# Expert tiles in pairs through Strassen's block product, in a Mamba and mixture-of-experts kernel

## The reference, cut to what matters

```python
E, TOP_K, D, M = 8, 2, 512, 1792
topk_w, topk_idx = jax.lax.top_k(router_probs, TOP_K)
topk_w = topk_w / jnp.sum(topk_w, axis=-1, keepdims=True)
x_rep_sort = jnp.take(x_flat, sort_idx // TOP_K, axis=0)      # rows sorted by expert
h = jax.lax.ragged_dot(x_rep_sort, w1, group_sizes)           # [8192, 512] x [512, 1792]
h = jax.nn.silu(h) * jax.lax.ragged_dot(x_rep_sort, w3, group_sizes)
out_sort = jax.lax.ragged_dot(h, w2, group_sizes)             # [8192, 1792] x [1792, 512]
out = jnp.einsum('tkd,tk->td', out_rep, topk_w)
```

## Time and profile before

| what | value |
|---|---|
| three runs, us | 4488.01, 4486.12, 4482.16; median 4486.12 |
| profiled execution: span from first to last instruction | 4487.7 us; no time of its own is listed beside the span |
| PE busy | 4104.8 us, 91% |
| DVE busy | 2421.6 us, 54% |
| ACT, POOL busy | 1941.3 us, 1849.3 us |
| mean granted clock of TensorE | 0.964 |
| last phase | from 2440.8 us, the first weight load |

### The profile page before, as it was taken

The page is one execution under the profiler, slowest core; times in us unless marked ns, Lnnn a source line. Parts: engine busy times, 40 slices in busy tenths (PEclk is TensorE's granted clock), DMA queues, the critical chain, the costliest instruction groups (busy, mean ns, idle before and its releaser), DMA issues. The chain is left out here.

```text
span 4487.7 us, 70319 instructions
## 1 busy us (share of the span) xinstructions
PE 4104.8 (91%) x25764; PEld 3331.3 (74%) x25764; DVE 2421.6 (54%) x3215; ACT 1941.3 (43%) x4096; POOL 1849.3 (41%) x1394
## 2 busy tenths in 40 slices
PE   6677889989898889898976999999999999999998
PEld 5565677767777677777764888888888888888887
DVE  5999999999999999999994000000000000000000
ACT  7677777877777777777761000000000000000000
POOL 3667777887787777876862000000000000000000
PEclk8888999999999999999987999999999999999999
DMA  4112454454535454545344113030301303030300
GB/s 155 63 61 67 143 163 159 126 168 158 173 117 166 160 170 122 162 157 177 106 141 158 30 25 101 14 112 14 112 14 20 107 14 112 14 112 14 112 14 12
DMA packets 289338, 452.00 MB, mean 101 GB/s; under 512 B 15856, under 2 KB 183408, under 8 KB 280816
## 3 DMA queue, kind: packets, MB, share of 16 engines
q1 hardware_dynamic: 272928, 413.27, 28.2%
q0 software_dynamic: 14768, 34.41, 4.1%
q10 hardware_dynamic: 1440, 1.81, 0.1%
HBM read 920.96 MB, written 45.95 MB: 215 GB/s over the span
## 5 line engine op out<-in xcount | busy, mean ns | idle before, releaser
L625 POOL TENSOR_TENSOR hs<-hs,bc 128x1024 f32<-128x1024 f32 x512 | 1215.1, 2373 | 308.7 <-DVE hs L1337 286.7
L1337 DVE TENSOR_TENSOR_SCAN hs<-dA,pU 128x1024 f32<-128x1024 f32 x512 | 1168.6, 2282 | 49.4 <-ACT dA L744 27.1
L1822 ACT ACTIVATE gate<-pA 128x512 f32<-128x512 f32 x216 | 117.5, 544 | 1859.9 <-PE pB L1860 1859.9
L1738 POOL DMA_INDIRECT out<-ow,trow x54 | 83.7, 1551 | 1967.3 <-DVE ow L1908 1967.3
L744 ACT ACTIVATE dA<-delta,aneg 128x255 f32<-128x255 f32 x2048 | 852.4, 517 | 37.4 <-DVE hs L1337 35.1
L1860 PE MATMUL pA<-xT,w1s 128*128 128x128 f32 x6048 | 799.7, 275 | 0.7 <-ACT xT L1831 0.7
L1860 PE MATMUL pB<-xT,w3s 128*128 128x128 f32 x6048 | 799.5, 275 | 0.0
L1136 PE MATMUL pY<-ident,hs 128*128 128x128 f32 x4096 | 565.1, 286 | 237.0 <-POOL hs L625 236.6
L1860 PEld LDWEIGHTS pA<-xT,w1s 128*128 128x128 f32 x6048 | 741.0, 192 | 26.4 <-issue 25.4
L1136 PEld LDWEIGHTS pY<-ident,hs 128*128 128x128 f32 x4096 | 487.8, 147 | 344.3 <-POOL hs L625 170.4
L1860 PEld LDWEIGHTS pB<-xT,w3s 128*128 128x128 f32 x6048 | 736.9, 192 | 0.0
(11 more groups left out here) (285 smaller groups left out, 3596.5 us busy)
## 6 DMA issues: line engine op xcount, KB each, us to landing
w1s<-in_w SPq DMA_DIRECT2D x165, 1024.0 KB
w3s<-in_w SPq DMA_DIRECT2D x165, 1024.0 KB
w2s<-in_w SPq DMA_DIRECT2D x165, 1024.0 KB
ew<-in_w SPq DMA_DIRECT2D x273, 512.0 KB, 4.1
win<-in_w_in SPq DMA_DIRECT2D x128, 512.0 KB, 4.7
bc<-bc_d SPq DMA_DIRECT2D x64, 1024.0 KB, 11.0
w1s<-in_w SPq DMA_DIRECT2D x55, 512.0 KB
w3s<-in_w SPq DMA_DIRECT2D x55, 512.0 KB
```

The source lines that it names most:

```text
L625: pool.tensor_tensor(hs[b][:, :, :], hs[b][:, :, :], bc[:, N + g * PN:N + (g + 1) * PN, :], ALU.mult)\
L1337: dve.tensor_tensor_scan(hs[b][:, :, :].rearrange("p n t -> p (n t)"), dA[b][:, :, :].rearrange("p n t -> p (n t)"), pU[:, :, :].rearrange ...
L1822: act.activation(gate[q % 2][:, 0:n, :], pA[q % 2][:, 0:n, :], ACT.Silu).then_inc(silu, 1)
```

## The change

With more than one tile of an expert left, two tiles (256 rows) are computed together by Strassen's product in Winograd's form. The matrices are cut in two by two blocks. Up, for each of `JN` = 7 steps of 256 hidden columns: the left matrix has w1's part above w3's, each cut at half of D; the right one has the two tiles, cut the same way. Down: the hidden halves by tile against w2, cut at 128 hidden rows and at half of D. Seven block products take the place of eight, and 15 block sums are added: four on each operand, seven on the products.

- VectorE makes the sums on weights (`combine_up`, `combine_down`; some in place, so w3s and w2s are overwritten and every pair reloads its expert's weights), the seven sums out of PSUM (`gather`, once for each step up and once down), and silu(h) times the other half (`multiply`).
- GpSimd makes the sums on the hidden values (`combine_h`) and on the turned rows (`combine_x`), and issues two indirect DMAs a pair.
- ScalarE copies the first product M1 out of PSUM, computes the silu in place in SBUF, and puts the row weights on the result.
- PSUM holds two sets of four banks: step j of the up part uses set j % 2, the down part set 1, the turned rows set 0.
- The last odd tile of an expert goes into a second loop behind all pairs, which works as the kernel before does, with its own semaphores and with weights loaded anew for each tile. Its first loads stand in SyncE's queue behind the whole last pair.
- The plan has two lists, pairs (at least 22, at most 29) and odd tiles (at most 8).

```diff
-NT_SURE = 2 * TOKENS // P - EARLY
-NT = NT_SURE + E - 1
+LEFT = 2 * TOKENS // P - EARLY
+NP_SURE = -(-(LEFT - E) // 2)
+NP_MAX = (LEFT + E - 1) // 2
+NPS = NP_MAX + 1
...
+KH, DH, JN = DC // 2, D // 2, MK // 2
+TURN_AFTER = 3
...
+            def combine_h(t, j):
+                k = JN * t + j
+                pool.wait_ge(h_mul, k + 1)
+                pool.tensor_tensor(hs[:, j, 0, :], hT[:, j, 2, :], hT[:, j, 3, :], ALU.add).then_inc(hs_step, 1)
...
+            def pair(t):
+                for j in range(JN):
+                    combine_h(t, j)
+                combine_x(t + 1)
+                add_rows(t)
...
+            def pair(t):
+                r, e, new = slot(t + 1)
+                for q in range(NQ):
+                    sp.wait_ge(up_mm, JN * t + min(2 * q + 2, JN))
+                    load_up(q, e, w13_in, new)
...
+                for q in range(NQ):
+                    sp.wait_ge(down_mm, JN * t + min(2 * q + 2, JN))
+                    load_down(q, e, w2_in, new)
+
+            each_pair(sp, n, pair)
...
+            r, e, new = slot(NPS)
+            sp.wait_ge(su_ready, n * NQ + NQ)
+            load_up(0, e, ow13_in, new)
...
+                for j in range(JN):
+                    if j % 2 == 0:
+                        pe.wait_ge(su_ready, NQ * t + j // 2 + 1)
+                    if j == 1:
+                        ge(pe, down_read, t)
+                    if j >= 2:
+                        pe.wait_ge(up_read, JN * t + j - 1)
+                    up(j)
+                pe.wait_ge(up_read, JN * t + JN - 1)
+                for j in range(JN):
+                    pe.wait_ge(h_ready, JN * t + j + 1)
+                    if j % 2 == 0:
+                        pe.wait_ge(td_ready, NQ * t + j // 2 + 1)
+                    down(j)
+                    if j == TURN_AFTER:
+                        pe.wait_ge(up_read, JN * t + JN)
+                        turn_rows(t + 1)
...
+            def combine_up(u, q):
+                lo, n = WCH[q]
+                cols = slice(lo, lo + n)
+                a11, a12 = w1s[:, 0:KH, cols], w1s[:, KH:DC, cols]
+                a21, a22 = w3s[:, 0:KH, cols], w3s[:, KH:DC, cols]
+                g = NQ * u + q
+                dve.wait_ge(w13_in[q], 32 * u + 32)
+                dve.tensor_tensor(su[:, 0, :, cols], a21, a22, ALU.add).then_inc(su_step, 1)
+                dve.wait_ge(su_step, 2 * g + 1)
+                dve.tensor_tensor(su[:, 1, :, cols], su[:, 0, :, cols], a11, ALU.subtract).then_inc(su_step, 1)
+                dve.tensor_tensor(a21, a11, a21, ALU.subtract)
+                dve.wait_ge(su_step, 2 * g + 2)
+                dve.tensor_tensor(su[:, 2, :, cols], a12, su[:, 1, :, cols], ALU.subtract).then_inc(su_ready, 1)
...
+                for j in range(JN):
+                    chunk(j)
+                    if j:
+                        multiply(j - 1)
+                    if isinstance(t, int) and j < NQ:
+                        combine_down(0, j)
...
+                    if j == 3:
+                        combine_up(t + 1, 0)
+                    if j == 5:
+                        combine_up(t + 1, 1)
+                multiply(JN - 1)
+                for q in range(2, NQ):
+                    combine_up(t + 1, q)
+                for q in range(2):
+                    combine_down(t + 1, q)
+                dve.wait_ge(h_mul, JN * t + JN)
+                dve.wait_ge(m1d_ready, t + 1)
+                ge(dve, added, 32 * t)
+                gather(DOWNS, m1d[:, :], d_step, t, ow, None, down_read)
+                for q in range(2, NQ):
+                    combine_down(t + 1, q)
```

More of the change, by code:

```diff
@@ L147, in spent @@
             return v if inner is None else v.rearrange("p (a e) -> p a e", e=inner)
-        tnum, over = spent(NT * E, E), spent(NT * E, E)
-        tn, ex, used, first = [spent(NT) for _ in range(4)]
-        ends, tiles, one8 = [spent(E) for _ in range(3)]
-        dbase, ci = spent(E + 1), spent(E).bitcast(I32)
+        tnum, over = spent(NSLOT * E, E), spent(NSLOT * E, E)
+        tn, ex, used, first = [spent(NSLOT) for _ in range(4)]
+        ends, pairs, odds, pair_end, odd_end, one8 = [spent(E) for _ in range(6)]
+        pair_base, odd_base = spent(E + 1), spent(E + 1)
+        ci, cp = spent(E).bitcast(I32), spent(E).bitcast(I32)
         pad = xf[:, :, :].rearrange("p t d -> p (t d)")[:, 0:RW]
@@ new lines, in add_rows @@
+            def add_rows(t):
+                pool.wait_ge(ow_ready, t + 1)
+                ge(pool, added, 32 * t)
+                pool.sem_inc(turn, 1)
+                for r in range(2):
+                    pool.indirect_dma_start(out=out, out_offset=bass.IndirectOffsetOnAxis(ap=trow[:, r:r + 1], axis=0),
+                                            in_=ow[:, 2 * r:2 * r + 2, :].rearrange("p h d -> p (h d)"), in_offset=None,
+                                            compute_op=ALU.add).then_inc(added, 16)
@@ L1864, in down @@
[L1864 removed]
+                    m.then_inc(oup_mm, 1)
+                turn_odd(t + 1)
+                pe.wait_ge(oow_ready, t + 1)
+                for q in range(NQ):
                     lo, n = WCH[q][0] // P, WCH[q][1] // P
[L1866 to L1867 removed]
+                    pe.wait_ge(oh_ready, NQ * t + q + 2)
+                    pe.wait_ge(ow2_in[q], 16 * t + 16)
                     for k in range(lo, lo + n):
[L1869 to L1870 removed]
@@ L1872, in tile @@
-                pe.wait_ge(x_copied, t + 1)
-                for q in range(NQ):
-                    up(q)
-                if not last:
-                    turn_rows(t + 1)
-                ge(pe, ow_ready, t)
-                for q in range(NQ):
-                    down(q)
-            turn_rows(0)
-            n = tiles_filled(pe)
-            tile(0, False)
-            with pe.Fori(1, NT_SURE) as t:
-                tile(t, False)
-            with pe.Fori(NT_SURE, NT - 1) as t:
-                with pe.If(t < n):
-                    tile(t, False)
@@ L1890, in _ @@
-            with pe.If(n > NT - 1):
-                tile(NT - 1, True)
+                        m = pe.matmul(pO[:, :], ohT[:, k, :], w2s[:, k, :], start=k == 0, stop=k == MK - 1)
+                    m.then_inc(odown_mm, 1)
+            n, odd = pairs_filled(pe), odds_filled(pe)
+            turn_rows(0)
+            each_pair(pe, n, pair)
+            pe.wait_ge(down_read, n)
+            turn_odd(0)
+            each_odd(pe, odd, odd_tile)
         @block.vector
         def _(dve):
-            def tile(t):
-                dve.wait_ge(x_in, 16 * t + 16)
-                ge(dve, added, 16 * t)
-                dve.tensor_copy(trow[:, :], xr[:, TOKCOL:TOKCOL + 1])
-                dve.tensor_copy(wrow[:, :], xr[:, WCOL:WCOL + 1]).then_inc(meta, 1)
+            def combine_up(u, q):
[11 more added lines that the diff above has]
+                dve.tensor_tensor(su[:, 2, :, cols], a12, su[:, 1, :, cols], ALU.subtract).then_inc(su_ready, 1)
@@ new lines, in gather @@
+            def gather(s, first, step, at, to, third, last):
+                u2, u3, u4 = [ut[:, i, :] for i in range(3)]
+                dve.tensor_tensor(u2, part(s, M6), first, ALU.add).then_inc(step, 1)
+                dve.tensor_tensor(to[:, 0, :], part(s, M2), first, ALU.add)
+                dve.wait_ge(step, 2 * at + 1)
+                dve.tensor_tensor(u4, part(s, M5), u2, ALU.add)
+                dve.tensor_tensor(u3, part(s, M7), u2, ALU.add).then_inc(step, 1)
+                dve.wait_ge(step, 2 * at + 2)
+                c12 = dve.tensor_tensor(to[:, 1, :], part(s, M3), u4, ALU.add)
+                if third is not None:
+                    c12.then_inc(third, 1)
+                dve.tensor_tensor(to[:, 2, :], part(s, M4), u3, ALU.add)
+                dve.tensor_tensor(to[:, 3, :], part(s, M5), u3, ALU.add).then_inc(last, 1)
```

462 lines of the change are left out of this document (324 added, 138 removed).

## The result

| kernel | median us (shortest to longest) | ratio to before, 95% interval |
|---|---|---|
| before | 4484.97 (4482.16 to 4488.01, 4 runs) | 1 |
| after | 4305.41 (4296.68 to 4306.74, 4 runs) | 0.9593, 0.9582 to 0.9604 |
| after, once more beside the experiments | 4305.95 (4300.94 to 4308.81, 5 runs) | 0.9603, 0.9590 to 0.9616 |

The ratios are those of the record, from all runs, and differ from the quotient of the medians by up to 0.0007. The kernel is 180 us faster. The forecast was 4291; the median lies 14 us above it and inside the likeliest case's range (4278 to 4315). The profiled execution has a span of 4302.6 us against 4487.7 before: 185 less, where the working gave 195. The granted clock is 0.957 in the mean.

What follows compares the result with a forecast made beforehand. TensorE's own instructions were taken to bound the last phase. 216 us off for 24 pairs, less 8, 10.6, 1.5 and 0.5, made 195 off 4487.7: 4292.7, as a median 4291 us; range 4278 to 4400.

Steps and rivals of the forecast that it cites:

- likeliest case: Whole kernel: TensorE bounds the pairs and the other work hides; 4278 to 4315 us, chance 0.60.
- first pair and plan: Start of last phase: first pair saves 1 us instead of 9, 8 lost; plan's extra small VectorE instructions cost 0.5.
- turn: gap and half clock: From pairs to odd tiles: TensorE stands 10.6 us (5 to 14) for loads; clock at half, up to 2 more.
- end of the kernel: Sum and scatter after the last tile: claimed to stay as before.
- A pair: TensorE in the last phase: 65.9 us a pair against 74.9 for two tiles, 9.0 off, 216 for 24.
- the lock: VectorE instructions with two SBUF inputs and GpSimd's SBUF-reading ones exclude each other; adds 0 to 15.8 us a pair to VectorE.
- The stall: Time a pair loses to VectorE and GpSimd excluding each other: bounds 0 and 5.9 us, taken as 0.
- Reserve: VectorE's sums end before TensorE needs their buffers; least reserve about 2 us, 1.9 ahead of step 6.
- A: Pairs: VectorE becomes the bound because of GpSimd; 4315 to 4440 us, chance 0.30.
- B: Pairs: VectorE and GpSimd exclusion plus falls of TensorE's clock; 77.2 us a pair, kernel 4564, slower; chance 0.04.
- C: Pairs: 11.5 MB of loads a pair are the bound; 89 us a pair, kernel 4850, slower; chance 0.02.
- D: Whole change: it does not do what it says, against 7 x 4 up products a step; given nothing.

## Why the prediction was right, step by step

The mechanism was right: TensorE alone sets the pace of the pairs, the sums and the reloads hide. What was off are two sizes of the sum, the turn above all. In the profile the sum compares as follows:

| term | predicted | measured |
|---|---|---|
| 23 pairs behind the first, against 46 tiles | 23 x 9.0 = 207 off | 23 x (74.94 - 65.80) = 210.2 off |
| first pair and plan | 1 off, 0.5 on | 2.0 on, 1.0 of it a later start |
| turn: gap and half clock | 10.6 + 1.5 on | 18.8 + 2.7 on |
| six odd tiles | 37.5 each | 37.47 each |
| end of the kernel | 0 | 1.2 on |
| in no term | | 0.5 on |
| together | 195 off | 185 off |

- **A pair.** 65.9 against 65.80. 0.1117 and 0.216 us an instruction were right; the transposes take 0.88. The measured gain is 9.14 and not 9.0, 0.10 of it from the shorter pair and 0.04 since two tiles are 74.94.
- **VectorE** was forecast at 56.0 us of work, at 62 with all of the lock less overlaps, against busy 1077.57 x 65.80 / 1300 = 54.5. I had named 85 to 95% busy as a sign of being right, and it is 83. Overlaps shorten the busy time, and the lock's 4.9 us are in it: half of the 10.3 that I called likeliest at most. My 10.3 added GpSimd's whole time to VectorE's; in the rows above a sum that takes 0.46 alone stretches VectorE's instruction by 0.14 to 0.25 us only. The stall was taken at 0, and it is 0, with less load to hide than I had given it.
- **Reserve.** Step 4's sums end at 3026.82 + 0.41 = 3027.23, step 6 starts at 3028.56: 1.3 us instead of 1.9, the chunk's four sums having taken 5.3 us instead of 4.8. Under three added sums most of the loss came by another chain, VectorE's multiplication through GpSimd's queue to the turned rows. I had looked at it (62 to 64 against 65.9) and set it aside, because I costed GpSimd at 15.8 us a pair.
- **GpSimd** is busy 645.61 x 65.80 / 1300 = 32.7 us a pair, twice the estimate. 0.46 us for a 128-wide sum was right where it is alone; the median of line 1824 is 0.90. The rest is waiting for VectorE inside the instruction, which the profile shows as busy. Nothing else needs GpSimd, so it cost nothing.
- **DMA.** 183 GB/s in the mean, forecast about 175; no wait of TensorE for weights or of the pairs' sums for loads in the steady part.
- **First pair.** Pair 1's first product is at 2530.45 (2991.05 less seven pairs) where the third tile began at 2528.4: it comes 2.0 us later, where I had a gain of 1. One of these three is the start: the first transposes are at 2450.51, before at 2449.52. The other two are the clock for the most part, 1.7 of them in step 6 as shown above. In the other profile of the changed kernel, without the fall, the product is at 2527.34, and the pair gains the 1 us of the forecast. So the term was right in one profile and 2 us short in the other. The step that was off in both is the end of VectorE's sums on w1 and w3. I had 2465.5; line 2120's last begins at 2469.24 (2467.75 in the other profile), since the sums wait for chunks to land (2.01 and 1.59 us, `w3s`). Step 6 then waits 2.0 us (2.6).
- **The turn** is the mis-sized term, 9.4 us against a net 10 that are missing (18.8 counts from where TensorE's next start would have been; from the modelled end of its last product it is 18.6). "The first odd loads are issued at its end" was wrong: SyncE first goes through five skipped iterations, its reads and waits, 5.2 us from TensorE's last product to the first issue, for which I had nothing. The loads, 1.35 us of issuing, then rows behind them in 10.1 us, were 11.4 instead of 9.4; the rows' part of it was 7.2 in other profiles, so part of this miss is chance. Transposes and copy at half clock are 2.0 instead of 1.1. Half clock in the first odd products: 4062.61 to 4090.35 is 27.7 us, against 28 groups of 0.893, or 25.0, so 2.7 instead of up to 2:

```profile
4060.61 1.09 PE L2072 MATMUL ps<-ident,xr 128*128 128x128 f32 x4 [16.59 <-DMA xr<-rows_d]
4062.61 2.07 PE L2085 MATMUL ps<-xT,w1s 128*128 128x128 f32 x8 [0.92 <-ACT xT L1994]
...
4090.35 0.60 PE L2072 MATMUL ps<-ident,xr 128*128 128x128 f32 x4
4127.82 0.60 PE L2072 MATMUL ps<-ident,xr 128*128 128x128 f32 x4
```

- **The end**: from the scatter's issue (4291.91, before 4478.12) to the end of the span 10.7 us instead of 9.5. Behind it the engines close two loops' semaphores instead of one. I had taken it as unchanged; whether that is the cause was not tested.
- **The rivals.** A (VectorE the bound through the lock) did not happen, but was near. Half of its sign is there, VectorE's sums of 1.22 us stretched to 1.36 to 1.47, and the other half, TensorE's waits ahead of steps 2 and 6, comes with one product less (60.09 a pair instead of 56.5). B and C did not: clock 1.00 and no DMA wait in the pairs. D fell with the page's counts.

## What to carry to other kernels

Trading products for sums pays as long as the chain of the sums fits under TensorE's shortened time at each place where a buffer is wanted again, so place the sums on a clock instead of comparing totals: here VectorE was at 83% with 1.3 us to spare at the tightest place, and one product less a step moved the bound. Where a second loop follows a first, price the queue that fills it, iteration by iteration, behind the last real one: it stands wholly on the path, with the landing of its loads (9.5 to 10.1 us in most profiles for the rows, 7.2 to 7.8 in three) and the clock that falls meanwhile. And follow a chain through the queue of a second engine (VectorE's product, GpSimd's queue, the turned rows) as carefully as the direct one.
